# A graph layer of 49 rounds and 49 units: blocks of nodes and chunks of edges from the last one down, with a cap on the units of a round

## What is computed

```python
msg = concatenate([x[src], edge_attr], axis=1) @ W1 + b1        # 50000 x 96 -> 128
agg = segment_sum(msg, dst, num_segments=100000)                # sums over the edges of a node
y   = concatenate([x, agg], axis=1) @ W2 + b2                   # 100000 x 192 -> 64
out = layernorm(x + y, axis=-1)                                 # (v - mean) / sqrt(var + 1e-5)

dst = minimum((100000 * uniform(50000) ** 2).astype(int32), 99999)   # then sorted, src in its order
```

## Time and profile before

| | us |
|---|---|
| time, median of 3 runs | 1054.15 |
| lowest and highest of them | 1051.51, 1056.91 |
| span of the profiled execution | 801.0 |
| median less span | 253.15 |
| PE busy in the span | 615.5 (77%) |
| DVE busy | 522.7 (65%) |
| POOL busy | 423.9 (53%) |
| ACT busy | 398.6 (50%) |
| mean granted TensorE clock | 0.843 of full speed |

### The profile page before, as it was taken

How to read it: one execution, slowest core, us unless ns; L and a number is a source line. 1 busy time by engine, 2 the same in 40 slices (tenths; PEclk the granted TensorE clock), 3 DMA queues, 4 the chain that set the end, 5 groups by cost and what they waited for, 6 DMA issues and landing times. The chain is left out here.

```text
span 801.0 us, 29016 instructions
## 1 busy us (share of the span) xinstructions
PE 615.5 (77%) x8418; PEld 544.4 (68%) x8419; DVE 522.7 (65%) x1826; ACT 398.6 (50%) x2012; POOL 423.9 (53%) x514
## 2 busy tenths in 40 slices
PE   1345445677778888888898898989898888878785
PEld 1344435566767777777777787878777777768675
DVE  3670111354465648858887788788787787878876
ACT  0011122102234344444567777777777777757655
POOL 5676766711676766475467777767466445200000
PEclk9655555657688779979999999999999999989988
DMA  2121222200223233333345545555455455533432
GB/s 63 28 37 36 37 37 34 57 9 12 61 54 82 59 86 79 79 78 79 100 110 139 127 122 139 129 136 147 115 139 144 110 132 134 134 86 115 126 97 81
DMA packets 168753, 71.47 MB, mean 89 GB/s; under 512 B 61570, under 2 KB 162447, under 8 KB 168720
## 3 DMA queue, kind: packets, MB, share of 16 engines
q1 hardware_dynamic: 104592, 51.74, 22.7%
q0 software_dynamic: 12544, 12.87, 8.5%
q10 hardware_dynamic: 51584, 6.41, 5.1%
HBM read 45.37 MB, written 25.60 MB: 89 GB/s over the span
## 5 line engine op out<-in xcount | busy, mean ns | idle before, releaser
L363 POOL DMA_INDIRECT feat<-in_x,src_now x392 | 393.6, 1004 | 255.4 <-issue 94.6
L775 DVE TENSOR_SCALAR onehot<-node_of_col,group_base,dst_of 128x256 bf16<-128x256 bf16 x952 | 287.4, 348 | 106.1 <-issue 78.9
L473 PEld LDWEIGHTS ps_y<-z_window,onehot 128*128 128x128 bf16 x5712 | 202.6, 101 | 65.8 <-DVE z_window L778 46.0
L473 PE MATMUL ps_y<-z_window,onehot 128*128 128x64 bf16 x5712 | 226.7, 198 | 26.6 <-DVE z_window L778 23.5
L574 ACT ACTIVATE square<-ps_y 128x64 bf16<-128x64 f32 x784 | 162.7, 239 | 135.8 <-PE ps_y L464 133.2
L574 ACT ACTIVATION_READ_ACCUMULATOR square<-ps_y 128x1 f32 x784 | 159.5, 224 | 0.0
L539 ACT ACTIVATE feat_t<-ps_t 97x512 f32<-97x512 f32 x98 | 58.6, 598 | 179.8 <-PE ps_z L400 159.9
L400 PE MATMUL ps_z<-wz,feat_t 97*128 97x64 f32 x784 | 123.1, 324 | 24.6 <-DVE z_rest L700 24.5
L400 PEld LDWEIGHTS ps_z<-wz,feat_t 97*128 97x128 f32 x784 | 118.0, 238 | 33.2 <-DVE z_rest L700 31.8
L392 PE MATMUL ps_t<-ident,feat 128*97 128x128 f32 x392 | 72.3, 333 | 86.8 <-DMA feat<-in_x,src_now 63.7
L464 PE MATMUL ps_y<-wx,x_t 128*128 128x128 f32 x784 | 118.4, 296 | 13.1 <-issue 8.7
(11 more groups left out here) (107 smaller groups left out, 226.2 us busy)
## 6 DMA issues: line engine op xcount, KB each, us to landing
xin<-in_x SPq DMA_DIRECT2D x97, 256.0 KB
out<-yout SPq DMA_DIRECT2D x97, 256.0 KB
feat<-in_x,src_now POOLq DMA_INDIRECT x392
feat<-in_edge_attr ACTq DMA_DIRECT2D x97, 64.0 KB
z<-in_src SPq DMA_DIRECT2D x1, 192.0 KB
z<-in_dst SPq DMA_DIRECT2D x1, 192.0 KB
xin<-in_x SPq DMA_DIRECT2D x1, 128.0 KB
out<-yout SPq DMA_DIRECT2D x1, 128.0 KB
```

The source lines that it names most:

```text
L363: nc.gpsimd.indirect_dma_start(out=feat[h][:, half * CB + c, 0:C], out_offset=None, in_=x[:, :], in_offset=bass.IndirectOffsetOnAxis(ap=sr ...
L473: mm = nc.tensor.matmul(ps_y[h][:, col:col + C], onehot[h][:, g, s, a, :], z_window[h][:, g, s, part * C:(part + 1) * C], start=False, sto ...
L775: ins = nc.vector.tensor_scalar(onehot[h][:, g, s, :, :], node_of_col[:, :, :], base, dst_of[:, bass.ds(firsts[g] + (at + s), 1)], ALU.add ...
```

## The change

The kernel goes through both lists from their end. Block b of the program is now the nodes from (97 - b) x 1024 on, and chunk c is chunk 390 - c of the edges: the index tables `src_idx`, `dst_of`, `least_row` and `most_row` are copied from PSUM in reverse order, `group_base` and `block_base` count down, and x, out and edge_attr are addressed from the top. The block with the cut end (nodes 99,328 to 99,999) and the cut chunk come first instead of last, so their loads and stores move to the start of the programs of SP and ACT, with one more clearing of a buffer on POOL. The formulas for `first`, `need` and `lacking` are as they were. Behind them stands a cap: `open_block` is the smaller of itself and 2.125 times the number of the round, so that at most 1.06 units open up for each round. One semaphore that nobody waits for (`x_go`) is counted up before each load of x.

```diff
@@ constants
 LAG = 2
+AHEAD = 2.125
@@ sync
-            sp.wait_ge(s_clear, 7)
+            sp.wait_ge(s_clear, 8)
+            whole, cut = tail_parts(x)
+            sp.dma_start(xin[0][0:TAIL_PARTS, TAIL_GROUPS, :], cut).then_inc(x_cut_loaded, 16)
...
-            with sp.Fori(2, PAIRS - 2) as k:
+            with sp.Fori(2, PAIRS - 1) as k:
+                top = sp.snap(BLOCKS - 2 * k)
                 for h in range(2):
-                    load_x(k + 1, h, x_blocks[2 * k + 2 + h])
-                store_round(k - 1)
+                    load_x(k + 1, h, x_full[top - (3 + h)])
+                store_round(k - 1, top + 1)
@@ gpsimd
+            nc.gpsimd.memset(xin[0][:, :, :], 0.0).then_inc(s_clear, 1)
...
-            nc.gpsimd.iota(group_base[:, :], pattern=[[GN, BLOCKS * G]], base=0, channel_multiplier=0,
+            nc.gpsimd.iota(group_base[:, :], pattern=[[-BN, BLOCKS], [GN, G]], base=(BLOCKS - 1) * BN, channel_multiplier=0,
-            nc.gpsimd.iota(block_base[:, :], pattern=[[GN, G]], base=0, channel_multiplier=BN,
+            nc.gpsimd.iota(block_base[:, :], pattern=[[GN, G]], base=(BLOCKS - 1) * BN, channel_multiplier=-BN,
...
+            nc.gpsimd.iota(round_no[:, :], pattern=[[0, 1]], base=0, channel_multiplier=1,
@@ vector
-            nc.vector.tensor_copy(dst_of[:, :], ps_t[1][:, 0:CHUNKS]).then_inc(s_dve, 1)
-            nc.vector.tensor_copy(src_idx[:, :], ps_t[0][:, 0:CHUNKS]).then_inc(s_idx, 1)
-            done[0] += 1
+            nc.vector.tensor_copy(src_idx[:, 0:LAST_CHUNK + 1], ps_t[0][:, LAST_CHUNK::-1])
+            nc.vector.tensor_copy(src_idx[:, LAST_CHUNK + 1:CHUNKS], ps_t[0][:, LAST_CHUNK + 1:CHUNKS])
+            nc.vector.tensor_copy(dst_of[:, 0:LAST_CHUNK + 1], ps_t[1][:, LAST_CHUNK::-1])
+            nc.vector.tensor_copy(dst_of[:, LAST_CHUNK + 1:CHUNKS], ps_t[1][:, LAST_CHUNK + 1:CHUNKS]).then_inc(s_idx, 1)
...
-                link(nc.vector.tensor_copy(row[:, :], bank[:, 0:CHUNKS]))
+                nc.vector.tensor_copy(row[:, 0:LAST_CHUNK + 1], bank[:, LAST_CHUNK::-1])
+                link(nc.vector.tensor_copy(row[:, LAST_CHUNK + 1:CHUNKS], bank[:, LAST_CHUNK + 1:CHUNKS]))
...
             link(nc.vector.tensor_scalar(open_block[:, :], open_block[:, :], -1.0, float(BLOCKS), ALU.mult, ALU.add))
+
+            link(nc.vector.scalar_tensor_tensor(out=open_block[:, :], in0=round_no[:, :], scalar=AHEAD,
+                                                in1=open_block[:, :], op0=ALU.mult, op1=ALU.min))
             link(nc.vector.tensor_copy(units[:, :], open_block[:, :]))
             link(nc.vector.tensor_scalar(units[:, :], units[:, :], 1, None, ALU.arith_shift_right))
```

More of the change, by code:

```diff
@@ L256, in _ @@
                 sp.dma_start(b2c[32 * r:32 * r + 1, :], b2.rearrange("(o f) -> o f", o=1)).then_inc(s_wload, 16)
-            for h in range(2):
-                sp.dma_start(xin[h][:, :, :], x_blocks[h]).then_inc(x_loaded[h], 16)
+            sp.wait_ge(x_cut_loaded, 16)
+            sp.dma_start(xin[0][:, 0:TAIL_GROUPS, :], whole).then_inc(x_loaded[0], 16)
+            sp.dma_start(xin[1][:, :, :], x_block(1)).then_inc(x_loaded[1], 16)
             sp.wait_ge(s_steps, 2)
@@ L271, in load_x @@
                 wait_rounds(sp, x_used[h], k)
+                sp.sem_inc(x_go)
                 sp.dma_start(xin[h][:, :, :], src_ap).then_inc(x_loaded[h], 16)
             def free_yout(k, h):
-                wait_rounds(sp, out_stored[h], k, 16)
+                if not (isinstance(k, int) and k == 0):
+                    sp.wait_ge(out_stored[h], 16 * k + (16 if h == 0 else 0))
                 sp.sem_inc(yout_free[h])
@@ L285, in store_round @@
                 for h in range(2):
-                    store(k, h, out_blocks[2 * k + h])
+                    store(k, h, out_full[top - h])
             for h in range(2):
@@ L290, in _ @@
             for h in range(2):
-                load_x(1, h, x_blocks[2 + h])
+                load_x(1, h, x_block(2 + h))
             for h in range(2):
-                load_x(2, h, x_blocks[4 + h])
-            store_round(0)
-            with sp.Fori(2, PAIRS - 2) as k:
-                for h in range(2):
-                    load_x(k + 1, h, x_blocks[2 * k + 2 + h])
-                store_round(k - 1)
[L299 to L305, removed]
-            store_round(PAIRS - 2)
[L307 to L316, removed]
+                load_x(2, h, x_block(4 + h))
+            for h in range(2):
+                free_yout(0, h)
+            sp.wait_ge(out_ready[0], 2)
+            whole, cut = tail_parts(out)
+            yt = yout[0][:, :, :].rearrange("p (g a) c -> p g (a c)", g=G)
+            sp.dma_start(whole, yt[:, 0:TAIL_GROUPS, :]).then_inc(out_stored[0], 16)
+            sp.dma_start(cut, yt[0:TAIL_PARTS, TAIL_GROUPS, :]).then_inc(out_stored[0], 16)
+            store(0, 1, out_block(1))
+            with sp.Fori(2, PAIRS - 1) as k:
+                top = sp.snap(BLOCKS - 2 * k)
+                for h in range(2):
+                    load_x(k + 1, h, x_full[top - (3 + h)])
+                store_round(k - 1, top + 1)
+            store_round(PAIRS - 2)
+            store_round(PAIRS - 1)
+            sp.wait_ge(out_stored[0], 16 * (PAIRS + 1))
+            sp.wait_ge(out_stored[1], 16 * PAIRS)
         @block.gpsimd
@@ L363, in gather @@
                     nc.gpsimd.indirect_dma_start(
-                        out=feat[h][:, half * CB + c, 0:C], out_offset=None, in_=x[:, :],
+                        out=feat[h][:, half * CB + feat_slot(c), 0:C], out_offset=None, in_=x[:, :],
                         in_offset=bass.IndirectOffsetOnAxis(ap=src_now[h][:, c:c + 1], axis=0)).then_inc(gathered[h], 16)
@@ L526, in _ @@
                 for_units(pe, mybir.EngineType.PE, k - LAG, unit)
-            edge_round(PAIRS - 1, loads=2)
+            edge_round(PAIRS - 1)
             for_units(pe, mybir.EngineType.PE, PAIRS - 1 - LAG, unit)
@@ L599, in _ @@
                 act.sem_inc(squared[h])
[L600 to L604, removed]
+            act.wait_ge(s_clear, 8)
+            load_ea_first()
+            load_ea(0, 1)
+            act.wait_ge(s_const, 13)
             nc.scalar.activation(std_eps[:, :], eps[:, :], ACT.Sqrt)
```

54 lines of the change are left out of this document (35 added, 19 removed).

## The result

The changed kernel takes **1110.46 us** (median of 3 executions, 1110.41 to 1110.63) against 1054.15 before: a ratio of 1.052, 95% interval 1.047 to 1.057. The forecast was 1355 us, in a range of 1325 to 1400. The direction was right and the size far off, and the place of the error is narrow: the span forecast for the changed kernel was 1102 us and its trace has 1108.5, but the measured time is only 2 us longer than that span, not 253.

The account below looks back on a forecast made before the run. POOL's gathers were taken to bind first, then DVE; an all-zero table ends their overlap. Rounds 600 + units 492.4 + 8.4 gave 1101, small edits 1102, plus 253 outside the span: 1355 us, range 1325 to 1400.

Parts of the forecast that it names:

- What bounds the kernel: POOL's gathers bind up to 148 us, 11.56 us a round; then DVE binds at 8.19 us a unit, overlapping rounds.
- The table is all zero: Table of units: an empty group in the reversed first block zeroes all entries but the last; all 49 units follow round 48.
- The rounds alone, 600 us: Rounds without units, paced by POOL at 5.78 us a half round: DVE's first one-hot starts at 600 us.
- The small edits: Extra memset, copies, cut-row load and backwards PSUM reads at the start: 1 us in all, span 1102.
- The units alone, 492.4 + 8.4: The 49 units behind the rounds, in DVE's time: 492.4 us, plus 8.4 for PE's trailing and the last squares, scale and store.
- The clock rival: PE at its lower clock binds the units, 12.2 us a unit: time 1538 us; chance 3%.
- from span to time: Outside the instructions: the median's 253.15 us over the span stays unchanged, so 1102 + 253 = 1355 us.
- The sign that the prediction named for this step: In the profile after: a median that is not 253 us over the span would fell the step from span to time.
- the part outside grows with the span: Rival: the time outside the span scales with it, giving 1450 us; chance 3%.
- The first rival: The table is not zero: 1.06 units run per round, span some 700 us, time 953 us; chance 4%.

Follow-up runs that it names:

- before, short code: Kernel before with assertions, without second and further steps of a block on PE and DVE (edges beyond a group's first two chunks left out): 739.62 us fast, 934.38 slow.
- mended, in pairs: Changed kernel with assertions, `first` set to 0 for a group without an edge, table rounded down to multiples of 2: 820.84 us fast, 1023.35 slow.
- e2: Kernel before with assertions, all entries of its table of units but the last multiplied by 0, order not reversed: 1114.89 us.
- f2: Changed kernel with assertions, `first` set to 0 for a group without an edge, cap kept: 758.55 us against 801.79 for the kernel before.
- g1: Changed kernel with only the run-time assertions added, at the fast level: 1107.00 us against 801.83 for the kernel before, ratio 1.381.
- e1: Kernel before with run-time assertions on each table value that an engine reads, nothing else, at the slow level: 1070.69 us.
- f1: Kernel before with the same run-time assertions, run again at the fast level: 830.74 us, ratio 1.036 to the kernel before.

## Why the prediction was wrong, point by point

The kernels that ran at both levels, with the number of units that follow the code of a round on PE ("steps"), counted in their traces, and the "issue" time of the pair sums in the slow trace:

| kernel | steps | fast, us | slow, us | difference | per step | "issue", slow |
|---|---|---|---|---|---|---|
| before | 34 | 802 | 1058, 1032 | 256, 230 | 7.5, 6.8 | no trace |
| before with assertions | 34 | 830.7 | 1070.7 | 240 | 7.1 | 177.8 |
| before, short code | 34 | 739 | 934.4 | 195 | 5.7 | 157.4 |
| mended | 45 | 758.6 | 1072.1 | 314 | 7.0 | 252.3 |
| mended, in pairs | 25 | 821 | 1023.4 | 202 | 8.1 | 104.5 |
| the change | 1 | 1107.0 | 1110.5 | 3.5 | | none |

(The last row's fast kernel has the assertions, its slow one not.)

- **What bounds the kernel: right for the trace, not for the time.** The trace showed the fast level, 801 us, and the median, 1054, was of the slow one. No row of the trace holds the 6 to 8 us of each step from a round to a unit.
- **The table is all zero: right.** No one-hot before 613 us, and e2 gives the same time without the reversal. A mended `first` (f2) brings the overlap back: 758.55 us against 1107.00 (g1).
- **The rounds alone, 600 us: 14 short.** POOL's half round took (593.3 - 14) / 98 = 5.9 us in the mean, where I carried one quiet stretch's 5.78 forward 82 times, and the way from POOL's end to the first one-hot was 20.5 instead of 18.2. The small edits cost 1.0 us as forecast: POOL's first `src_now` started at 14.39 instead of 13.35.
- **The units alone, 492.4 + 8.4: 6 long, in part by luck.** 8.18 for the plain ones was exact. The seven two-step ones took 13.14 and not 13.85, 5 us less in all. Unit 47, which I took from unit 1 at a lower clock (0.76 in 209 to 230 us of the trace before), took 13.7 and not 20.8. Unit 48 took 46.4 us, up to the end of DVE's scaling of unit 47, where I had 41.4: its clock was 0.63, and the 3 us that I took off were not there. The last two errors cancel in part.

```profile
1039.69 0.60 DVE L811 TENSOR_SCALAR onehot<-node_of_col,group_base,dst_of 128x256 bf16<-128x256 bf16 x2 [0.35 <-issue]
...
1053.43 0.60 DVE L811 TENSOR_SCALAR onehot<-node_of_col,group_base,dst_of 128x256 bf16<-128x256 bf16 x2 [0.39 <-issue]
```

(DVE's timeline of the changed kernel, the first one-hots of units 47 and 48.)
- **The clock rival:** wrong; in the unit stretch from 700 to 925 us the granted clock was 1.00, the 2.4 GHz level, with PE busy for 202 of 225 us. The section of the Trainium skill that the prediction names (TensorE: Matmul & The Clock Gate, "HAM oscillation — how this bites in real kernels") tells of a kernel whose clock falls in long waits for DMA between its bursts. I read it as if any wait would do. PE's only waits in this stretch were 137 for DVE's copies, 0.2 us at most, and nothing of the kind happens. The rounds alone agree with the section: there PE waited up to 5.9 us for gathers, and the clock was 0.50 in the first trace, with durations to match (g1 has the same durations under its recorded 1.00).

```profile
700.00:925.00 225.00, 202.06 (x3363) 168.04 (x3360) 194.90 (x744) 156.79 (x1015) 0.00 (x0) 1.00 0.45 127
...
PE ps_y L498 <- DVE z_window L814: 21.6, 137, 0.2
```

(A sum by stretch, columns as in the earlier trace rows, and the waits on PE in that stretch.)
- **The step that failed: from span to time.** I took the 253.15 us for something outside the instructions that stays, as the section on the time before says too, although no row showed it. It is inside: the timed executions of the kernel before were another 250 us longer than the profiled one, most of it in stalls whose number goes with how often PE passes from a round's code to a unit's. The changed kernel does so once, and so it loses the overlap (some 300 us by the fast level, 1107 against 802) and sheds the stalls (230 to 256). What is left at the slow level is 56. The sign that the prediction named for this step came: a median that is not 253 us over the span. The rival "the part outside grows with the span" doubted the same step, but in the wrong direction; that the change could take the 253 us away was not among my cases. A span of 1102 with a time of 1104 would have been within 0.6% of the result.
- **The first rival's size:** a table that isn't zero was forecast at a span of 700; f2 has 757.8. A unit with its round took 11.6 us in the mean up to unit 37, less than the 12.2 forecast, but the first one-hot came at 72.9 us, where the sum counted from 13; so unit 37 ended at 514 instead of 477. The units with second steps (38 to 46) took 152 us with their rounds, for 142 forecast. The rest is at the end: DVE waited behind unit 47 for the last round until 703.9, and then the last unit, with the densest blocks, worked alone:

```profile
518.00:705.00 187.00, 145.79 (x2334) 126.27 (x2334) 136.07 (x504) 82.89 (x413) 73.80 (x87) 0.91 0.31 75
705.00:757.00 52.00, 34.16 (x434) 28.13 (x434) 25.00 (x86) 5.96 (x37) 0.00 (x0) 0.60 0.08 21
```

(Sums by stretch of f2, columns as in the earlier trace rows.) In the old order that unit ran while gathers went on.

**What stays open.** That PE's instructions come late at this step is what "issue" and the matmuls that come singly suggest, and the rough proportion to the number of steps supports it, but no run shows what the sequencer waits for. In the pairs kernel the pair sums' "issue" time covers only half of the difference. The other engines have more idle time labelled "issue" at the slow level too: DVE 225.6 us in e1 against 102.3 in f1, POOL 142.1 against 95.6. In the changed kernel DVE has 177.3 us of it at the slow level and 50.8 at the fast one, at nearly the same time. Whether these are late instructions as well, or only waits with another label, isn't shown. What sets the level isn't known either: it held through each job, and the same chip had both. Whether a shift of the code's place matters at the slow level wasn't tried.

## What to carry to other kernels

Where the profiled span and the median differ by much more than the first and last few microseconds, the trace is of an execution that the median isn't: a sum made from it can be right in each term and still not be added to that median. Reversing or reordering a list moves its odd last entry (here a group of nodes past the end, whose "first chunk" is a clamped default) to where everything waits for it, so recompute each default by hand for the new position. And interleaving two code bodies can have a price for each change between them that one execution shows and another hides. Fewer and larger turns trade it against idle engines: against the kernel beside it, the paired kernel was at 0.992 and the unpaired at 1.013 at the slow level, some 2% won, and at 1.023 and 0.940 at the fast one, some 8% lost.

## What the runs showed of the hardware that I had not expected

One program took 802 us in 20 executions of three jobs and 1028 to 1065 us in 21 of two others, within 1.2% in each job, and both levels came on one chip. At the slow level, matmuls of TensorE came mostly 0.73 us apart (some 1.44), in the timelines shown of the unpaired kernels from the 25th or 26th pair sum of the first block behind a round on, for about 8 us, waiting for nothing that the profile shows; at the fast level the same 48 took 1.56 us. In two executions of the changed kernel the records give TensorE a clock of 0.50 and of 1.00 in the rounds alone, and 16 of its products took 3.52 and 3.51 us there, so a mean granted clock has to be read beside the durations. The run-time assertions, 576 more instructions in the execution (29,592 against 29,016), cost 29 us at the fast level (830.7 against 801.8) and 13 at the slow one (1070.7 against 1058.1).
